# A two-attention, eight-expert block on one core: half-sized expert tiles, a re-weighted work order, layer norms without a centring product, and row maxima kept as one 16-bit word

## What the reference computes

```python
h = layernorm(x) * (1 + ca) + sa                     # ca, sa, ... per item, from a small product
x = x + ga * attention(h, position bias)             # 16 heads of 8, all keys visible
h = layernorm(x) * (1 + cb) + sb
# second block on h:
h2 = h + causal_attention(rmsnorm(h) * g1, rotary)   # 16 heads of 8
y  = h2 + moe(rmsnorm(h2) * g2)                      # 8 experts, best 2 per token, hidden 384
x  = x + gb * y
# moe: out = sum over the token's 2 experts of weight * (silu(x @ wg) * (x @ wu)) @ wd
```

## Time and profile before

| what | value |
|---|---|
| median of the runs | 887.95 us |
| the profiled execution's own time | 892.79 us |
| its span, first to last instruction | 890.9 us |
| granted TensorE clock, mean | 0.975 |
| PE, DVE, ACT, POOL busy | 88%, 69%, 61%, 35% |

### The profile page before, as it was taken

One profiled execution on the slowest core, in us unless ns is written; L12 is line 12 of the kernel. 1 busy time (PEld: TensorE's weight loads), 2 busy tenths in 40 slices (PEclk: granted clock), 3 DMA queues, 4 the chain that ended last, 5 costly groups with the idle time before them and its releaser, 6 DMA issues.

```text
span 890.9 us, 36166 instructions
## 1 busy us (share of the span) xinstructions
PE 788.3 (88%) x15115; PEld 482.6 (54%) x15115; DVE 616.6 (69%) x1534; ACT 543.4 (61%) x961; POOL 316.2 (35%) x449
## 2 busy tenths in 40 slices
PE   6879789989999998988898899998999999759995
PEld 4334445544554554445444556556566666639792
DVE  2564777698588687857867968678665875627773
ACT  3465477866767659576665765856567465315552
POOL 2082113331343234234324212444334563535451
PEclk9999899999999999999999999999999999779998
DMA  6996800000000000000000110011101111125624
GB/s 159 374 334 226 270 3 22 20 21 16 21 26 16 15 18 21 14 19 20 16 21 14 44 33 24 26 30 37 45 27 29 37 41 50 36 63 158 174 79 133
DMA packets 50575, 60.76 MB, mean 68 GB/s; under 512 B 6001, under 2 KB 36977, under 8 KB 50033
## 3 DMA queue, kind: packets, MB, share of 16 engines
q1 hardware_dynamic: 35152, 27.06, 10.6%
q10 hardware_dynamic: 10272, 21.14, 7.2%
q0 software_dynamic: 4992, 10.27, 3.4%
HBM read 22.79 MB, written 35.65 MB: 66 GB/s over the span
## 4 chain that ended last, share of the span: by engine, by line
PE 37%; DVE 22%; issue 14%; DMA 10%; POOL 7%; ACT 7%; SPq 1%; POOLq 0%; DVEq 0%; ACTq 0%
DVE row_max L1347 11%; PE ps L945 8%; DMA slot_rows<-rows,slots 6%; POOL eo_rows L1669 5%; PE ps L772 5%; PE ps L805 5%; PE ps L783 3%; PE ps L828 2%; PE ps L819 2%; PE ps L1031 2%; PE ps L811 1%; ACT stage L1184 1%; ACT probs L1184 1%; DMA eo_rows<-eo_t,to_t 1%; PE ps L903 1%
## 5 line engine op out<-in xcount | busy, mean ns | idle before, releaser
L1347 DVE TENSOR_REDUCE row_max<-ps 128x4 f32<-128x1024 f32 (+1 forms) x256 | 267.1, 1075 | 62.0 <-PE ps L783 42.8
L1184 ACT ACTIVATE probs<-ps 128x1024 f32<-128x1024 f32 x128 | 131.1, 1028 | 45.7 <-PE ps L805 44.0
L1669 POOL DMA_INDIRECT eo_rows<-eo_t,to_t x92 | 89.7, 975 | 100.8 <-ACT eo_t L1235 70.2
L772 PE MATMUL ps<-bias_t,ch 64*32 64x512 f16 x2048 | 106.4, 388 | 19.1 <-DVE row_max L1347 8.8
L1184 ACT ACTIVATE stage<-ps 128x1024 f32<-128x1024 f32 x96 | 97.2, 1030 | 21.3 <-PE ps L811 20.5
L1655 POOL DMA_INDIRECT slot_rows<-rows,slots x64 | 64.8, 1013 | 103.5 <-DMA slot_rows<-rows,slots 64.2
L1023 PE MATMUL ps<-xT_t,wgu_hi 128*128 128x256 f16 x276 | 77.9, 282 | 9.2 <-DVE row_max L1347 4.1
L945 PE MATMUL ps<-probs,v_pad 128*32 128x256 f32 x1024 | 82.3, 391 | 2.3 <-ACT probs L1184 1.8
L1502 DVE SCALAR_TENSOR_TENSOR gate_s<-gate_t,ps 128x256 f32<-128x256 f32 x138 | 57.0, 413 | 37.7 <-ACT gate_t L1229 37.4
L1229 ACT ACTIVATE gate_t<-ps 128x256 f32<-128x256 f32 x138 | 52.6, 386 | 46.9 <-PE ps L1025 41.1
L772 PEld LDWEIGHTS ps<-bias_t,ch 64*32 64x32 f16 x2048 | 29.6, 89 | 89.4 <-issue 39.9
(11 more groups left out here) (165 smaller groups left out, 1534.2 us busy)
## 6 DMA issues: line engine op xcount, KB each, us to landing
slot_rows<-eo_g ACTq DMA_DIRECT2D x1, 12642.0 KB, 51.2
slot_rows<-eo_g ACTq DMA_DIRECT2D x1, 7998.0 KB, 26.7
x_t<-slot_rows SPq DMA_DIRECT2D x46, 129.0 KB, 2.6
eo_g<-eo_rows SPq DMA_DIRECT2D x16, 256.0 KB, 3.4
xT<-in_x SPq DMA_DIRECT2D x16, 128.0 KB, 2.1
kept<-resid SPq DMA_DIRECT2D x16, 128.0 KB, 1.7
resid_b<-kept SPq DMA_DIRECT2D x16, 128.0 KB, 2.6
out_dram<-outT SPq DMA_DIRECT2D x16, 128.0 KB, 2.2
```

Of the source, the lines that this page charges most:

```text
L772: eng.matmul(ps[HR * c:HR * (c + 1), two[r], :].rearrange("p (j s) -> p j s", j=2), csth("flip")[half, :], bias_t[half, way, 2 * g:2 * g + ...
L1184: eng.activation(probs[a][:, 2 * (k % 2):2 * (k % 2) + 2, :], both_of("c%d" % a, i, "e%d" % k), ACT.Exp).then_inc(z["exp"], 1)
L1347: ins = eng.tensor_reduce(row_max[a][:, qt, 4 * g:4 * g + 4].rearrange("p (r j) -> p r j", r=2), of_heads, AX.X, ALU.max)
L1669: eng.indirect_dma_start(out=eo_rows, out_offset=bass.IndirectOffsetOnAxis(ap=to_t[:, done % 4, t:t + 1].bitcast(U32), axis=0), in_=eo_t[: ...
```

## The change

1. **Half tiles.** A tile is 128 rows; tiles are handled in pairs whose halves may belong to different experts. A pair has the 256 rows of an old tile, so every evaluation keeps its size except that gate and up products now have 128 columns each, twelve per chunk instead of six, each with its own weight load. The worst case falls to 24 pairs for part one and 16 for part two. TensorE's queue works out two column addresses per pair; SyncE loads two start rows and issues two DMAs per pair.
2. **Order.** The planner gets new durations, hop times by source and destination engine, a table `EARLY` of offsets (one per kind of operation, first and later items apart) added to the priority, a single priority number, and tiles of part one may use only banks 4 to 6 (`banks_for`).
3. **Expert weights.** They are loaded in 12 parts of 512 columns into memory of `hid`, spread over items 0 to 7, each scaled on ScalarE and split on GpSimd; the second attention's buffers no longer share memory with them, and f2 of item 0 no longer waits for the split.
4. **Layer norm.** `pe_centre` transposes instead; ScalarE subtracts the mean by its bias (-mean times rstd). GpSimd makes that bias with two more operations per norm.
5. **Row maxima.** `tensor_reduce` negates and writes the 16-bit word itself. The two "mx" operations and the remainder word are gone.

```diff
-TILE = 2 * P
+TILE = P
-N_TILE = [(2 * (e - s) * S + NX * (TILE - 1)) // TILE for s, e in PARTS]
+N_TILE = [-(-((2 * (e - s) * S + NX * (TILE - 1)) // TILE) // 2) for s, e in PARTS]
+TILES_FROM = 4
+EARLY = {"f1.ss": -15, "f1.root.n": -228, "f1.turn": 9, "f1.aff": 26, "f1.qk": -3, "f1.hi": -1, "f1.again": 2, "f1.q": 17982, "c1.v": 3,
...
-                return (3 if key[1] < N_PIECES else 2, -way[key], rank[key])
-            return (1 if key[1] else 0, -way[key], rank[key])
+                behind = 3 if key[1] < N_PIECES else 2
+            else:
+                behind = 3 if key[0] == "w" and key[2] != "v2" else 1 if key[1] else 0
+            return (round(1000.0 * behind - way[key] - (EARLY.get(kind(key), 0.0) if self.ops[key][0] else 0.0), 6), rank[key])
...
-                ins = eng.matmul(bank[:, t * D:(t + 1) * D], src[:, t * P:(t + 1) * P], cst("centre"), start=True, stop=True)
+                ins = eng.transpose(bank[:, t * D:(t + 1) * D], src[:, t * P:(t + 1) * P], ident)
...
-                    x_hi, x_lo = xT_t[:, done % 2, 0, :], xT_t[:, done % 2, 1, :]
-                    block = bass.ds(cols[done % 2] + c * P, P)
-                    for w in range(2):
-                        dst = bank[:, w * S:(w + 1) * S]
-                        eng.matmul(dst, wgu_hi[:, w, block], x_hi, start=True, stop=False)
-                        eng.matmul(dst, wgu_hi[:, w, block], x_lo, start=False, stop=False)
-                        ins = eng.matmul(dst, wgu_lo[:, w, block], x_hi, start=False, stop=True)
+                    for t in range(2):
+                        x_hi, x_lo = [xT_t[:, done % 2, k, t * P:(t + 1) * P] for k in range(2)]
+                        block = bass.ds(cols[done % 2][t] + c * P, P)
+                        for w in range(2):
+                            dst = bank[:, w * S + t * P:w * S + (t + 1) * P]
+                            eng.matmul(dst, wgu_hi[:, w, block], x_hi, start=True, stop=False)
+                            eng.matmul(dst, wgu_hi[:, w, block], x_lo, start=False, stop=False)
+                            ins = eng.matmul(dst, wgu_lo[:, w, block], x_hi, start=False, stop=True)
...
-                ins = eng.activation(xn["n%d" % a][:, t, :], held("f%d" % a, i, "centre")[:, t * D:(t + 1) * D], ACT.Copy,
-                                     scale=rstd["n%d" % a][:, t:t + 1])
+                ins = eng.activation(xn["n%d" % a][:, t, :], held("f%d" % a, i, "centre")[:, t * D:(t + 1) * D], ACT.Identity,
+                                     bias=less["n%d" % a][:, t:t + 1], scale=rstd["n%d" % a][:, t:t + 1])
...
-                    ins = eng.tensor_reduce(row_max[a][:, qt, 4 * g:4 * g + 4].rearrange("p (r j) -> p r j", r=2), of_heads,
-                                            AX.X, ALU.max)
+                    word = qk_tok[a][:, b, qt, 0, 4 * g:4 * g + 4, 3 * HD].rearrange("p (r j) -> p r j", r=2)
+                    ins = eng.tensor_reduce(word, of_heads, AX.X, ALU.max, negate=True)
                 ins.then_inc(z["max"], 1)
-            yield at("mx")
...
+                eng.tensor_scalar(minus[pre][:, :].unsqueeze(2), moments[pre][:, :, 0:1], -1.0, None, ALU.mult).then_inc(norm[pre]["v"], 1)
...
+            if pre[0] == "n":
+                eng.wait_ge(norm[pre]["root"], 2 * i + 1)
+                eng.tensor_tensor(less[pre][:, :], minus[pre][:, :], rstd[pre][:, :], ALU.mult).then_inc(norm[pre]["root"], 1)
...
         def sp_weights(eng):
-            yield 0.0
-            eng.dma_start(wgu[:, 0, :], wg_in).then_inc(s_moew, 16)
-            eng.dma_start(wgu[:, 1, :], wu_in).then_inc(s_moew, 16)
+            for n in range(N_PART):
+                k, cols = part_of_weights(n)
+                yield PLACE["w", n, "load"]
+                eng.wait_ge(x1_done, n // 2 + 2)
+                if n >= N_STAGE:
+                    eng.wait_ge(su["wsplit"], 2 * (n - N_STAGE + 1))
+                eng.dma_start(staged[:, n % N_STAGE, :], (wg_in, wu_in)[k][:, cols]).then_inc(s_moew[n % N_STAGE], 16)
```

More of the change, by code:

```diff
@@ L204, in back @@
         job = "b%d" % a
-        last = self.op((job, i, "byq"), "dve", 0.72, [("c%d" % a, i, "end")] + self.before(job, i), (), X)
-        last = self.chain(job, i, last, ("rec", "dve", 0.34), ("mul", "pool", 0.68), ("byd", "dve", 0.38))
-        return self.op((job, i, "out"), "pe", 0.45, [last] + free, ONE)
+        last = self.op((job, i, "byq"), "dve", 0.705, [("c%d" % a, i, "end")] + self.before(job, i), (), X)
+        last = self.chain(job, i, last, ("rec", "dve", 0.34), ("mul", "pool", 0.63), ("byd", "dve", 0.433))
+        return self.op((job, i, "out"), "pe", 0.46, [last] + free, ONE)
     def b1(self, i):
@@ L221, in h @@
     def h(self, i):
-        last = self.op(("h", i, "tok"), "pe", 0.8, [("b2", i, "h2")] + self.before("h", i), ONE)
-        last = self.op(("h", i, "rows"), "act", 0.5, [last, ("b2", i, "end")] + ([("h", i - 2, "end")] if i > 1 else []))
-        last = self.op(("h", i, "top"), "dve", 1.66, [last], (), "mine")
-        twice = self.op(("h", i, "twice"), "pool", 0.9, [last])
-        self.op(("h", i, "gap"), "act", 0.25, [last])
-        self.op(("h", i, "both"), "pool", 1.3, [last])
-        self.op(("h", i, "comb"), "dve", 0.5, [("h", i, "gap")])
@@ L229, in h @@
-        self.op(("h", i, "resid"), "pool", 1.4, [("b2", i, "h2")])
+        last = self.op(("h", i, "tok"), "pe", 0.62, [("b2", i, "h2")] + self.before("h", i), ONE)
+        last = self.op(("h", i, "rows"), "act", 0.62, [last, ("b2", i, "end")] + ([("h", i - 2, "end")] if i > 1 else []))
+        last = self.op(("h", i, "top"), "dve", 2.075, [last], (), "mine")
+        twice = self.op(("h", i, "twice"), "pool", 0.718, [last])
+        self.op(("h", i, "gap"), "act", 0.203, [last])
+        self.op(("h", i, "both"), "pool", 0.481, [last])
@@ L230, in h @@
+        self.op(("h", i, "comb"), "dve", 0.68, [("h", i, "gap")])
+        self.op(("h", i, "resid"), "pool", 1.752, [("b2", i, "h2")])
         self.op(("h", i, "kept"), "sp", 0.4, [("h", i, "resid")])
-        rank = self.op(("h", i, "rank"), "pe", 0.3, [("h", i, "both"), ("h", i, "comb")], ONE)
-        last = self.op(("h", i, "slot"), "dve", 1.0 if i + 1 not in [e for _, e in PARTS] else 3.0, [rank], (), "mine")
+        rank = self.op(("h", i, "rank"), "pe", 0.14, [("h", i, "both"), ("h", i, "comb")], ONE)
@@ L233, in h @@
+        last = self.op(("h", i, "slot"), "dve", 0.69 if i + 1 not in [e for _, e in PARTS] else 3.0, [rank], (), "mine")
         for q in range(2 * KT):
-            last = self.op(("h", i, "scatter%d" % q), "pool", 1.2, [last, twice] + ([("h", i - 1, "scatter3")] if i and not q else []))
+            last = self.op(("h", i, "scatter%d" % q), "pool", 0.98, [last, twice] + ([("h", i - 1, "scatter3")] if i and not q else []))
         self.op(("h", i, "end"), None, 2.0, [last])
     def weights(self):
-        last = ("f1", 0, "root.n1")
@@ L302, in run @@
         ready = {k: 0.0 for k, n in waits.items() if not n}
-        clock = {e: 0.0 for e in HOP}
+        clock = {e: 0.0 for e in ENGINES}
         mode, free, holder = 0, {}, {}
@@ L382, in run @@
                         continue
+                if eng == "pe" and self.ops[k][5] != mode:
+                    t = max(t, clock["pe"] + DRAIN)
+                t = round(t, 6)
                 if best is None or (t, line(k)) < best[:2]:
@@ L432, in schedule @@
             job(i)
-    p.op(("w", 0, "load"), None, 30.0)
+    for name, us in (("x", 7.7), ("mod", 13.7), ("bias", 22.6)):
+        p.op(("w", 0, name), None, us)
     p.weights()
@@ L620, in block_kernel @@
         s_x = [sem("s_x%d" % k) for k in range(3)]
-        s_moew = sem("s_moew")
+        s_moew = [sem("s_moew%d" % k) for k in range(N_STAGE)]
         s_bias = sem("s_bias")
@@ L1834, in constants @@
             km[row:row + 24, j] = 1
[L1835 removed]
+            ko[row + 24, j] = 1
     put("kmask", km)
```

257 lines of the change are left out of this document (137 added, 120 removed), and 13 rows, old and new, of the table EARLY.

## The result

The changed kernel takes 820.63 us (median of four runs, 817.09 to 822.63) and the kernel before, on the same chip, 888.59 (887.44 to 890.98). The ratio is 0.9228, 95% interval [0.9185, 0.9271]: 68 us less. The profiled execution took 818.75 us, its span 816.9 at a clock of 0.989. So its own time fell by 74.0 us from 892.8, where I had forecast 47. In the experiments, four of the ten runs of one kernel (the weights in parts) were over 1.5% above its fastest and are left out of its ratio.

The account below looks back on a forecast made before the run. TensorE was taken as the bound, busy 88% of the span. -12 + 1 - 8 + 3 - 5 - 12 - 14 = -47 us from 892.8 gave 845.8, less 4.8 for the median: 841 us, range 807 to 873.

Parts of the forecast that it names:

- rival 1: Order and shorter chains win more: D reaches -30 and C -15, 813 us; chance 0.17 (below 822).
- D: New order of the work from item 1 to 15: -12 us, bounds +15 and -30.
- The gap: From the last h2 (762.0 us) to the second part's first tile (791.6 us): routing and scatters, which no edit shortens.
- E: Half tiles in both parts: -22 us for fewer tiles, +8 us for dearer pairs, so -14 us.
- Rival 2: Register-addressed weight loads only half hidden: 0.078 us a product, +34 instead of +8, 867 us; chance 0.2 (858 to 882).
- A: Start of the kernel, weights in parts: -12 us (bounds 0 and -20), and +1 us for the small pieces.
- B: Layer norms, transpose for centring product: -8 us on PE, +3 us for two more GpSimd operations per norm.
- C: Row maxima: 21.8 us leave DVE and a step before the transposes goes; -5 us, bounds 0 and -22.

Follow-up runs that it names:

- the first set: Runs on one chip against the kernel before at 923.98 us: all edits but the order 1.0174, half tiles alone 1.0191, offsets emptied 1.0232.

## Why the prediction was right in direction and short in size

820.6 lies in the range (807 to 873), 20 us under the forecast of 841, and a hair below the bound of 822 that I had given rival 1, of chance 0.17. The sum came as near as it did by luck: two large errors of opposite sign met in it.

**D, the order, is the step that failed.** I gave it -12 us with a bound of -30; the runs give -78 on one chip, and the trace of the other has 21 + 15 + 14 = 50 us that fit it. The shorter chains could have a share in the idle time and the fillers, but with the old order they did not save any: 153 fillers of 49.8 us with all other edits, 152 of 46.1 with the half tiles alone, in the same set. The term failed in three ways. The pace: 38.2 us was read between items 2 and 4 and taken for "the long middle". The same rows give (762.03 - 145.23) / 15 = 41.1 for the mean, which already said that the later items were slower; the stretch from item 9 on ran at 48.6. The ceiling: "10% of 617 = 62, half of it" as the bound was a guess laid over a good number. Idle time and fillers together fell by 36 of 66 us. The gap: "no edit shortens it" was true, 29.6 us before and 29.4 after (687.90 to 717.29), but an order can fill it with pairs from the crowded stretch. Rival 1 put D at -30, at which I had stopped; its mechanism, a better order, is what happened.

**E, the half tiles, failed the other way: the price of their products.** I took 0.055 us a product and +8 us in all. Rival 2's number, 0.078, is what the chip does. The weight load that I thought might be half exposed is not; it is the address. Register work that doubles was named in my working, but its price, +8 us for all addresses and steps, was taken near the row of "tr", whose addresses are fixed; by 0.95 in place of 0.66 us for 120 chunks it is 35 us of PE's time, of which fixing the columns gives back 17. The PE timeline, first and last transposes of the sixteen pairs of part two, against the nineteen of the earlier trace rows:

```profile
717.29 0.39 PE L1060 MATMUL ps<-ch,x_t 128*128 128x128 f16 x4
...
787.15 0.38 PE L1060 MATMUL ps<-ch,x_t 128*128 128x128 f16 x4
```

Fifteen intervals in 69.86 us are 4.66 us a pair, where I had looked for 4.2. 16 x 4.66 = 74.5 us stand against 19 x 3.99 = 75.8: the second part gained 1 us, not 12. And that 1 us flatters the half tiles. The pace of 3.99, on which my sum rests, holds a start at half clock (0.50 from 791.6 to 796 us) and a stretch at 0.86 (820 to 830). From 833.66 to 863.47 us at a clock of 1.00 a tile took 29.81 / 8 = 3.73 us. The pairs ran at 1.00 throughout; ahead of them PE had been busy 25.7 of 29 us. With fixed columns the pair takes 4.18 (711.62 to 774.39 us in that trace), which is the 4.2 that I had looked for with the addresses in it: 0.055 us was right for the products, and what I had set aside for the addresses was far too little. In part one 24 x 4.66 = 112 us stand against 27 x 3.99 = 108 by the same pace. So E is about +3 us by these paces instead of -14. In the old order, on the two chips where the kernel before takes 924 and 927 us, it was +18 to +21. By the traces of the first set most of that is no misfit between plan and chip: PE idled no longer than with whole tiles, and a pair takes 4.98 us there against 4.02 for a tile, a larger difference than the 0.67 here. The last few us are not assigned.

The Trainium skill (TensorE: Matmul & The Clock Gate, "Back-to-back issue gap") gave about 81 ns for a load-and-matmul pair at 128 columns; the mean here is 79. Yet with fixed columns the same pairs run at 56 ns, load included. So the number fits and its reason, as a rate for every such stream, does not: the measurement decides for 56, and for a step of 0.06 us at a new register address where the queue has no lead.

**A, the start, was right in its steps and too large in its sum.** The second norm of item 0 starts 0.54 us after its x1 (8.3 before); timelines of DVE and PE:

```profile
62.48 0.48 DVE L1433 SCALAR_TENSOR_TENSOR x1T<-ps,modT,xT 128x256 f32<-128x256 f32 x1 [1.41 <-PE ps L1010]
63.02 0.44 PE L901 MATMUL ps<-cf,x1T 128*128 128x128 f32 x2 [0.58 <-DVE x1T L1433]
```

No DVE operation of 5 us is left there, where one took 4.89. But h2 of item 0 came at 135.8 us, not near 130, and alone on the old order the edit gives 4 us of the 11 forecast. The last item's end, not item 0's, sets the time. In that kernel's trace item 0's h2 is at 113.7 us, against 145.5 in the one with the half tiles alone (same planner, same chip), but item 1's at 176.1 against 179.8: by then nearly all of the lead is gone. Item 0's 135.8 in the changed kernel is thus no measure of A, for with the old order and all the other edits it was 117.6 (137.0 in the changed kernel on that chip): the new order spends that lead.

**B and C came near, but only in the new order.** B was forecast at -8 for PE and +3 for GpSimd; putting the product back costs 4 us, not clear of noise. A, B and C together had -21 in my sum, and in the old order they gave the 2 to 5 us named above. Shorter chains and a lighter PE are worth little where the order can't use them. The groups show the new operations (counts of 32 and 64; busy, mean ns), which answer to the earlier trace rows:

```profile
L1163 ACT ACTIVATE xn_n<-ps,less_n,rstd_n 128x128 f32<-128x128 f32 x64 | 26.1, 467 | 9.6 <-POOL less_n L1642 9.4
...
L1632 POOL TENSOR_SCALAR minus_n<-moments_n 128x2 f32<-128x2 f32 x32 | 7.1, 223 | 2.5
L1642 POOL TENSOR_TENSOR less_n<-minus_n,rstd_n 128x2 f32<-128x2 f32 x32 | 6.4, 199 | 2.5
```

GpSimd's two cost 0.42 us a norm, just below my lower bound of 0.46. What I had not priced is ScalarE: with a bias from memory its operation takes 467 ns instead of 380, 64 x 0.087 = 5.6 us; whether that costs any time was not tried. C was forecast at -5 and measured at 7. DVE's busy time fell by 28.5 us, where 22 and the 18 pairs of operations of six tiles (15) would give 37. The maxima themselves kept their duration, as assumed: 1221 ns where it was 1209.

**The chances.** Faster had 0.91, rightly. But the two terms that decided, D and E, were the ones whose price came from the least fitting rows: a window of the middle for the whole, and transposes with fixed addresses.

## What to carry to other kernels

Ahead of pricing a new order, cut the trace at every item, and look for the slow stretch and the empty gap near it: what an order can win is found there and not in the idle share of one window. A searched order belongs to its plan: here one duration changed, even towards the truth, cost 17 us, so search again after such a change; and edits that pay inside it can be worth little without it. Price products whose operand comes through a register by the queue as well as by TensorE, and use one address for as many columns as possible.

## What the runs showed of the hardware

- Twelve 128-column 16-bit products with a weight load each start 0.056 us apart if the addresses are constants. A new register address for every third product adds a step of some 0.06 us once the queue's lead is used up, so 0.24 in place of 0.17 us for three; with 256 columns a product, 0.33 us for three, no step is seen.
- An ACTIVATE of 128x128 fp32 from PSUM takes 467 ns with a scale and a bias that are read per partition, 380 as a Copy with the scale alone.
- Chips differ. The same kernel before took 888 to 891 us on two occasions and 924 and 927 us on two other chips, 4% more; the changed one 820.6 and 864.3, 5% more. The changed kernel's stretch from item 9 to 15 took 238.5 us on the first and 262.6 on the other, its pairs 4.66 and (833.48 - 755.75) / 15 = 5.18. Until item 9's h2 the two differ by 8 us only, in the rest, where the tiles run, by 38. The twelve starts of a chunk in both traces lie mostly 0.06 and 0.12 apart; on the slower chip there are more steps between them, and TensorE's waits on "issue" add up to 19.0 us against 6.5. VectorE too waits 16.9 us on "issue" ahead of L1550, where the faster chip has none, while single operations last the same (the maxima 1221 ns on both). What makes that chip's queues wait was not found, and whether the order is worth 78 us on the faster one too was not tried.
